# Attention and MLP block on one core: rows transposed into natural column order, and the queries' projection reading them with a step

## What is computed

```
xn   = layernorm(x)                                    # rows of 128
z    = layernorm(xn) * ln_g + ln_b
q, k, v = z @ Wq + bq, z @ Wk + bk, z @ Wv + bv        # 16 heads of 8
p    = sinusoidal_pe(512, 128) @ Wp
pos  = relative_shift((q + v_bias) @ p.T)              # 512 x 512 per head
attn = softmax(((q + u_bias) @ k.T + pos) * 8**-0.5)
out  = x + (attn @ v) @ Wo + bo + mlp([xn, -xn])       # MLP 256 -> 512 -> 512 -> 128, weights +-1
```

## Time and profile before

| | us |
|---|---|
| median of 3 runs | 1458.08 (1455.66 to 1462.42) |
| span of the profiled execution | 1453.5 |
| PE busy | 1441.7 (99%) |
| DVE busy | 1357.5 (93%) |
| ACT busy | 1226.6 (84%) |
| POOL busy | 754.8 (52%) |

### The profile page before, as it was taken

How to read it: one execution, slowest core, us unless ns; L and a number is a source line. 1 busy time by engine, 2 the same in 40 slices (tenths; PEclk the granted TensorE clock), 3 DMA queues, 4 the chain that set the end, 5 groups by cost and what they waited for, 6 DMA issues and landing times.

```text
span 1453.5 us, 41653 instructions
## 1 busy us (share of the span) xinstructions
PE 1441.7 (99%) x16170; PEld 977.4 (67%) x16170; DVE 1357.5 (93%) x3489; ACT 1226.6 (84%) x1365; POOL 754.8 (52%) x753
## 2 busy tenths in 40 slices
PE   8999999999999999999999999999999999999999
PEld 4566666666676666766666676666766666666666
DVE  6899999999999999999999999999999999999996
ACT  5688888888888898888888888888888888888874
POOL 5575555555655565454655555566554645543410
PEclk9999999999999999999999999999999999999999
DMA  5999999999999999999999999999999999999992
GB/s 197 385 399 394 383 404 386 389 391 379 409 377 399 394 386 397 377 399 383 397 398 373 408 376 397 397 377 407 382 391 392 384 398 380 394 380 389 396 397 108
DMA packets 80867, 550.41 MB, mean 379 GB/s; under 512 B 9376, under 2 KB 10528, under 8 KB 15136
## 3 DMA queue, kind: packets, MB, share of 16 engines
q1 hardware_dynamic: 43376, 278.61, 49.5%
q10 hardware_dynamic: 37296, 269.15, 47.9%
HBM read 274.57 MB, written 273.15 MB: 377 GB/s over the span
## 4 chain that ended last, share of the span: by engine, by line
PE 95%; DMA 2%; ACT 1%; DVE 1%; issue 0%; SPq 0%; ACTq 0%
PE ps_pt L853 35%; PE ps_av L867 19%; PE ps_pos L829 14%; PE ps_job L756 12%; PE ps_job L720 4%; PE ps_job L710 3%; PE ps_job L735 2%; PE ps_con L841 1%; PE ps_job L731 1%; DMA shift<-pos_sb 1%; ACT pt_sb L514 1%; PE ps_job L743 1%; PE ps_job L726 1%; DMA sc_sb<-shift 1%; DMA heads<-in_pe_t 0%
## 5 line engine op out<-in xcount | busy, mean ns | idle before, releaser
L673 DVE CUSTOM_DVE_ANT_0 sc_sb<-ps_con,sc_sb 128x512 f32<-128x512 f32 x1024 | 661.9, 682 | 65.0 <-PE ps_con L841 61.5
L500 ACT COPY pos_sb<-ps_pos 128x1024 f32<-128x1024 f32 x510 | 518.0, 1016 | 180.4 <-PE ps_pos L829 169.4
L681 DVE TENSOR_SCALAR sc_sb<-sc_sb,nmax 128x512 f32<-128x512 f32 x1024 | 629.2, 646 | 0.1
L853 PE MATMUL ps_pt<-c_sb,sc_sb 128*128 128x128 f32 x4048 | 553.5, 280 | 2.5 <-ACT pt_sb L514 1.5
L514 ACT ACTIVATE pt_sb<-ps_pt 128x1024 f32<-128x1024 f32 x506 | 519.1, 1026 | 20.1 <-PE ps_pt L853 18.8
L853 PEld LDWEIGHTS ps_pt<-c_sb,sc_sb 128*128 128x128 f32 x4048 | 433.9, 141 | 127.1 <-issue 93.2
L867 PE MATMUL ps_av<-pt_sb,v_sb 128*9 128x128 f32 x8192 | 319.9, 274 | 0.1
L867 PEld LDWEIGHTS ps_av<-pt_sb,v_sb 128*9 128x9 f32 x8192 | 172.8, 90 | 184.4 <-issue 182.2
L841 PE MATMUL ps_con<-k_stack,q_stack 26*128 26x512 f32 x1024 | 267.5, 496 | 1.8 <-DVE nmax L673 1.5
L396 POOL CAST h<-act_sb 128x512 fp32r<-128x512 f32 x128 | 78.1, 610 | 360.7 <-ACT act_sb L473 357.4
L829 PE MATMUL ps_pos<-p_stack,q_stack 26*128 26x512 f32 x1024 | 259.6, 496 | 1.2 <-ACT pos_sb L500 0.9
(11 more groups left out here) (116 smaller groups left out, 1015.8 us busy)
## 6 DMA issues: line engine op xcount, KB each, us to landing
shift<-pos_sb SPq DMA_DIRECT2D x256, 1026.0 KB, 9.3
sc_sb<-shift ACTq DMA_DIRECT2D x256, 1024.0 KB, 9.8
x_sb<-in_x SPq DMA_DIRECT2D x16, 256.0 KB, 11.8
out<-x_sb SPq DMA_DIRECT2D x15, 256.0 KB, 10.5
c_sb<-in_consts ACTq DMA_DIRECT2D x1, 288.0 KB, 6.8
sc_sb<-in_wp SPq DMA_DIRECT2D x1, 256.0 KB, 5.8
sc_sb<-in_stack_w ACTq DMA_DIRECT2D x1, 256.0 KB, 5.5
heads<-in_pe_t SPq DMA_DIRECT2D x1, 256.0 KB, 6.9
```

Source lines behind the costliest of these rows:

```text
L500: act.copy(to, ps_pos[:, :, :]).then_inc(s_pe, 1)
L673: dve.tensor_tensor_reduce(sc_sb[:, m % N_SC, t, :], ps_con[:, k, :], sc_sb[:, m % N_SC, t, :], -SCALE, 3.4e38, ALU.add, ALU.min, nmax[:, ...
L681: dve.tensor_scalar(sc_sb[:, m % N_SC, t, :], sc_sb[:, m % N_SC, t, :], nmax[:, m % N_SC, t:t + 1], None, ALU.subtract).then_inc(s_sub, 1)
L853: last = pe.transpose(pt_banks(k)[:, j % 2, t * P:(t + 1) * P], sc_sb[:, u % N_SC, t, j * P:(j + 1) * P], id_sb)
```

## The change

The order of the columns is turned round at another place. The transposes of TZ write `ps_job` with a step, so that PSUM holds the natural order; ACT evicts it contiguously, straight to `z_t`; POOL splits `z_t` instead of a buffer of `act_sb`; V and KG read `z_t` as before and wait for the eviction itself (`s_jev`) where they waited for the copy (`s_zt`). The copy at L522 is removed. The queries still come out in the partition order, so QG's moving operand, `z_hl` (and `z_q` in batch 0), is read as `d t q a`: its innermost step is 128 elements, that is 512 bytes, with 4 elements in it; then 32 at a step of 4 elements; then 4 at a step of 1. ACT gets a wait, ahead of the eviction of TZ, for the last KG of the batch before. TZ keeps its turn in the ring of `act_sb`, unused.

```diff
--- before.py
+++ after.py
@@ -231,6 +231,10 @@
             b, rest = divmod(h - half, 32)
             return b if rest == 0 and 2 <= b < B else None
 
+        def by_partition(rows):
+
+            return rows.rearrange("d (a q t) -> d t q a", a=4, t=NT)
+
         def unit(n, lag):
             return n - lag if 0 <= n - lag < UNITS else None
 
@@ -374,7 +378,7 @@
 
             def split(name, b, c):
                 k = ACTS[(name, b, c)]
-                src = act_sb[:, k % N_ACT, :]
+                src = z_t[:, :] if name == "TZ" else act_sb[:, k % N_ACT, :]
                 pool.wait_ge(s_jev, ev(name, b, c))
                 if name in ("QG", "KG"):
                     dst, low, ready = {"QG": (QS, LOW_Q, s_qs), "KG": (KS, LOW_K, s_ks)}[name]
@@ -448,9 +452,7 @@
                 if (name, b, c) == ("QG", 0, 0):
                     act.activation(QS[:, 0, :], BANK[(name, b, c)], ACT.Identity, bias=low_bias_q[:, 0:1],
                                    scale=LOW_Q).then_inc(s_low, 1)
-                    act.activation(z_t[:, :].rearrange("d (a q t) -> d t q a", a=4, t=NT),
-                                   BANK[("TZ", 0, 0)].rearrange("d (t q a) -> d t q a", a=4, t=NT),
-                                   ACT.Identity, bias=BB, scale=G).then_inc(s_zt, 1)
+                    act.activation(z_t[:, :], BANK[("TZ", 0, 0)], ACT.Identity, bias=BB, scale=G).then_inc(s_zt, 1)
                     return
                 if name in SPLITS:
                     wait(act, s_hl, ACTS[(name, b, c)] - N_ACT + 1)
@@ -460,7 +462,8 @@
                 elif name == "TH":
                     last = act.copy(o_t[:, :], ps_job[:, :])
                 elif name == "TZ":
-                    last = act.activation(dst, ps_job[:, :], ACT.Identity, bias=BB, scale=G)
+                    act.wait_ge(s_job, job("KG", b - 1, GROUPS - 1))
+                    last = act.activation(z_t[:, :], ps_job[:, :], ACT.Identity, bias=BB, scale=G)
                 elif name in ("QG", "KG"):
                     if b == 0 and name == "KG":
                         act.wait_ge(s_bias, 4)
@@ -515,12 +518,6 @@
                        .then_inc(s_exp, 1)
                 for j in taken(h):
                     take_job(*j)
-                for name, b, c in taken(h - 1):
-                    if name == "TZ" and b > 0:
-                        act.wait_ge(s_jev, ev("TZ", b))
-                        raw = act_sb[:, ACTS[("TZ", b, 0)] % N_ACT, :]
-                        act.copy(z_t[:, :].rearrange("d (a q t) -> d t q a", a=4, t=NT),
-                                 raw.rearrange("d (t q a) -> d t q a", a=4, t=NT)).then_inc(s_zt, 1)
 
         @block.vector
         def _(dve):
@@ -707,13 +704,16 @@
                         pe.wait_ge(s_whl, 1)
                         pe.wait_ge(s_hl, ACTS[("TZ", b, 0)] + 1)
                     cut = slice(c * P, (c + 1) * P)
-                    return [lambda i=i: pe.matmul(out, wq_hl[:, i // 2, cut], z_hl[:, i % 2, :], start=(i == 0), stop=(i == 2))
+                    return [lambda i=i: pe.matmul(out, wq_hl[:, i // 2, cut], by_partition(z_hl[:, i % 2, :]),
+                                                  start=(i == 0), stop=(i == 2))
                             for i in range(3)]
                 if name == "QG":
-                    return [lambda: pe.matmul(out, wq[:, c * P:(c + 1) * P], z_q[:, :],
+                    return [lambda: pe.matmul(out, wq[:, c * P:(c + 1) * P], by_partition(z_q[:, :]),
                                               start=True, stop=True)]
-                if name in ("KG", "V"):
-                    pe.wait_ge(s_zt, b + 1)
+                if name in ("KG", "V") and b == 0:
+                    pe.wait_ge(s_zt, 1)
+                elif name in ("KG", "V"):
+                    pe.wait_ge(s_jev, ev("TZ", b))
                 if (name, b) == ("V", 0):
                     pe.wait_ge(s_c2, 16)
                 if name == "KG":
@@ -727,6 +727,8 @@
                 if name in ("T1", "TZ", "V", "TO", "TH", "TY"):
                     def block(t):
                         dst, cut = out[:, t * P:(t + 1) * P], slice(t * P, (t + 1) * P)
+                        if name == "TZ":
+                            dst = by_partition(out)[:, t, :, :]
                         if name == "V":
                             return pe.matmul(dst, z_t[:, cut], w_sb["v"], start=True, stop=True)
                         if name == "TO":
```

## The result

The changed kernel takes 1496.31 us (median of 4 runs, 1493.19 to 1496.66); the kernel before, in runs beside it, 1456.87. The ratio is 1.026, 95% interval 1.0233 to 1.0286: slower by 2.6%. Forecast were 1494 us and a price of 36 us. The medians lie 39.4 us apart; the profiled span grew from 1453.5 to 1491.4 us, by 37.9, and it is this growth that the traces can take apart.

What follows compares the result with a forecast made beforehand. PE was taken to bound the kernel. QG's stepped read added 36 us, all other terms 0: 1453.5 + 36 = 1489.5 us of span, with 4.6 us more 1494 us (+2.5%). Range 1454 to 1535 us; the forecast's own 1484 to 1506.

Steps and rivals of the forecast that it cites:

- Bound by PE: Whole kernel: the sum of PE's pieces is the time; ACT's work counts only where PE waits for it, 18 us.
- The copy at 0: Removing ACT's copy (15 x 1159 ns = 17.4 us) gains 0, covered by ACT's slack; practical end 3 us.
- Rival D: PE's 18 us of waits on ACT shrink by half and the step is free: 1449 us; chance 0.03.
- QG's stepped read at +0.20 us a pass, 36 us: 180 QG passes in PE's chain fall to the float32 pass's pace; bounds 0 and 104 us.
- ACT's ratio of 2.0: Second estimate for QG's stepped read, from ACT's stepped against contiguous copy, 1159/582: 0.23 x 1.0 x 180 = 41 us.
- Nothing hides this term.: Longer QG jobs delay values and next positions directly, 60 times; DVE, 83.6 of 87.6 us busy, follows PE.
- Batch 0 at 0: QG's 8 stepped float32 passes cost 0, upper end 4.6 us; ACT's L451 saves 0.5 us at most, taken 0.
- Transposes at 0: TZ's 60 stepped PSUM writes fit their pace of 0.11 us each and cost 0; upper end 6.6 us.
- rival C: Stepped PSUM writes of TZ's transposes are slow as well: +6.6 us on the forecast, 1501 us; chance 0.12.
- Rival B: QG's stepped read costs more than double: 1513 to 1562 us; signs +0.3 us a pass, job past 1.6 us; chance 0.18.
- Rival A: The step is free for PE, QG pass stays 0.23 us: 0 to -3 us, 1457 us; chance 0.29.
- The 4.6 us between the profiled span and the median: Whole run: median 1458.1 us exceeds the profiled span by 4.6 us, added unchanged to the forecast span.

Runs made afterwards that it cites:

- e7: Changed kernel with plain transposes and plain QG reads in all batches, so against the kernel before only ACT's copies are gone: 1455.33 us, ratio 0.9993.
- e9: Kernel before with three more plain passes added to each QG of batches 1 to 15, results overwritten: 1487.02 us, ratio 1.0207.
- e10: Kernel before with one more plain pass added to each QG of batches 1 to 15: 1461.23 us, ratio 1.0034.
- e3: Changed kernel with plain transposes and plain QG reads in batches 1 to 15, batch 0 still stepped: 1458.77 us, ratio 1.0031 to the kernel before.
- e1: Changed kernel with QG reading plainly in batches 1 to 15, stepped transposes kept: 1460.27 us, ratio 1.0035 to the kernel before.
- e4: Changed kernel with another reading order of z_hl in each of a batch's four QG jobs; one run, 1480.86 us, total time not used.

## Why the prediction was right, point by point

- **Bound by PE.** Right: each part that lengthened a PE piece lengthened the run, and taking 17 us from ACT did nothing (e7).
- **The copy at 0.** Right, 0.9993 (0.9978 to 1.0009). Rival D, ACT's relief, is excluded beyond the 3 us that the interval leaves. One reading on the way was loose: ACT's next copy of positions starts at 75.59, before the record of the copy ends at 75.74, and most of the copy lies in the half before the one that was looked at; that half takes 2.94 us as well.
- **QG's stepped read at +0.20 us a pass, 36 us.** The mechanism was right, the size too small, and the reason given for it wrong. It measured +0.253 us a pass, 45.6 us. "If a stepped read can supply one column where the contiguous one supplies two, a QG pass falls to that pace" took the float32 pass for a floor; but float32 passes double as well, 0.43 to 0.91 us. The better neighbour was the one put second, ACT's ratio of 2.0 for the same order, which gave 41 us; the measured ratio is 2.1. "Half the pace" would also have been 41 us and not "the same 36": half the pace of a 0.23 us pass adds 0.23, not 0.20.
- **"Nothing hides this term."** Wrong. DVE's 4 us of slack in a batch was a mean over halves; in single halves DVE was late and PE waited. 8 to 10 us of added PE time are absorbed by that (e9, e10). The error had the other sign from the one above, and that is luck: without it the sum would be 1453.5 + 45.6 + 3.8 + 4.6 = 1507.5 us, just outside the forecast's own range of 1484 to 1506. With it the sum came out within 3 us: 45.6 + 3.8 - 11.5 = 37.9. The 11.5 is what was left over; by the table it is 7.2 in the L756 halves, 2.7 up to the 17th half (+1.1 where batch 0 adds 3.8, inside the scatter of that stretch), 1.2 in the QG halves (+44.4 for 45.6) and 0.4 elsewhere.
- **Batch 0 at 0.** Wrong, "already at the slower pace": some 0.96 us a job, 3.8 us of PE; e3 and e7, each against the kernel before beside it, differ by 3.9 us (1458.77 - 1454.8 and 1455.33 - 1455.28). ACT's part was right: L451 fell from 1271 to 767 ns.
- **Transposes at 0**, and rival C. Right: 0.44 us, and e1 and e3 the same. The Trainium skill, "Advanced Engine Details and Errata", section "Memory Cachelines", says that any non-contiguous PSUM pattern slows matmuls significantly; here float32 writes with a 512-byte innermost step ran at full pace, at 128 and at 512 columns. Its rule for SBUF, two hits in a 16-byte line for full performance, has the right direction, but two hits weren't enough (e4: 1.33 us in pairs, 1.35 at a step of two, against 0.69). The measurements decide.
- **Rival B** is excluded by its own signs, though its name, "more than double", is just true at 2.1: 0.253 us a pass, under its 0.3, and 1.45 us a job, under its 1.6. **Rival A** is excluded by the result.
- The 4.6 us between the profiled span and the median was no fixed surrounding: the runs of the changed kernel lie 1.8 us above their own spans. The rest is the scatter between executions.

## What to carry to other kernels

A reordering is free or dear by where its step stands. Here it cost nothing on the PSUM side, whether PE wrote with it in float32 or ACT read with it, and about a doubling on the SBUF side, for PE's moving operand and its weights; ACT's write took 1.6 times as long (L451) or double (L522). Put it on the side of an engine that isn't the bound, and look at what runs beside it: POOL, half idle, slowed DVE. And before work is taken from an engine, look in the chain for a piece that ends on it; 17 us of ACT were worth nothing, and of the chain only 1% was ACT's.

## What the runs showed that I had not expected

- PE comes near its plain pace only in runs of four columns of 4 bytes: 0.81 us for a job of three passes in runs of four, 1.33 in pairs, 1.35 at a step of 2, 1.38 at 4, 1.45 at 128, 0.69 plain.
- Stepped weight loads: 329 ns against 192.
- POOL: cast 1.14 us against 0.61, subtraction 1.60 against 1.30, with a stepped source; a pair of DVE subtractions 2.22 us beside them against 0.88 with POOL idle and 1.77 to 2.04 beside plain splits.
- Why runs of four matter, and whether an fp32r pass (twice the pace of float32) could write PSUM with a step for nothing, stays open; the second wasn't tried.
